# Attention and expert kernel: start-up transfers, an integer block count, a re-ordered last batch and a last block in halves

## The reference

```python
x = layernorm(x + attention(x))          # x: 8 batches of 512 tokens, 128 wide
x = layernorm(x + experts(x))
# attention, 16 heads of 64: linear, no softmax
q, k, v = split(x @ W_qkv);  q, k = relu(q @ W_f + b_f), relu(k @ W_f + b_f)
out = (q @ (k^T @ v)) / (q . sum(k) + 1e-6);  return out @ W_out + b_out
# experts: 8, two for each token, hidden width 512
p, i = top_2(softmax(x @ gate_w^T))
return sum over the two of  p * (gelu(x @ w1[i] + b1[i]) @ w2[i] + b2[i])
```

## Time and profile before

| | |
|---|---|
| median of 3 runs | 463.35 us (462.35 to 464.86) |
| profiled execution | 462.59 us, span 460.8 us |
| busy share PE, DVE, ACT, POOL | 93%, 71%, 60%, 35% |
| chain that ended last | PE 77%, DVE 11% |

### The profile page before, as it was taken

One profiled execution on the slowest core, in us unless ns is written; L12 is line 12 of the kernel. 1 busy time (PEld: TensorE's weight loads), 2 busy tenths in 40 slices (PEclk: granted clock), 3 DMA queues, 4 the chain that ended last, 5 costly groups with the idle time before them and its releaser, 6 DMA issues.

```text
span 460.8 us, 8851 instructions
## 1 busy us (share of the span) xinstructions
PE 429.2 (93%) x2784; PEld 342.2 (74%) x2784; DVE 325.5 (71%) x946; ACT 274.4 (60%) x538; POOL 162.3 (35%) x164
## 2 busy tenths in 40 slices
PE   6989999999999999999999979889999999999940
PEld 5876776776776776776776647569999999999840
DVE  3574968969968968969968997755874433456786
ACT  2664766756756756756656636339555565555565
POOL 2011101431431431431431402425777655555550
PEclk9899999999999999999999999999999999999985
DMA  8980220210210210210100060499696899499534
GB/s 221 303 213 0 71 68 1 74 43 2 69 43 6 70 41 7 68 43 7 60 29 7 24 230 24 142 310 297 192 245 217 280 359 302 130 355 329 165 125 137
DMA packets 40013, 61.16 MB, mean 133 GB/s; under 512 B 6287, under 2 KB 27284, under 8 KB 39840
## 3 DMA queue, kind: packets, MB, share of 16 engines
q1 hardware_dynamic: 30560, 49.65, 34.4%
q0 software_dynamic: 4544, 8.54, 5.3%
q10 hardware_dynamic: 4864, 2.42, 1.8%
HBM read 44.55 MB, written 17.49 MB: 135 GB/s over the span
## 4 chain that ended last, share of the span: by engine, by line
PE 77%; DVE 11%; issue 3%; DMA 3%; ACT 2%; ACTq 1%; POOL 1%; SPq 1%; POOLq 0%; DVEq 0%
PE psO L575 11%; PE psA L465 9%; PE psA L466 9%; PE psA L467 9%; PE psG L705 7%; PE psA L554 6%; PE psS L705 4%; PE psG L465 3%; PE psA L622 3%; PE psG L566 3%; PE psG L466 3%; PE psG L467 3%; PE psG L597 2%; PE psS L511 1%; DMA rn<-expert_rows 1%
## 5 line engine op out<-in xcount | busy, mean ns | idle before, releaser
L425 POOL DMA_INDIRECT expert_rows<-rows,pos x64 | 62.1, 970 | 95.9 <-PE psA L467 67.0
L450 POOL DMA_INDIRECT expert_results<-q_act,kT x56 | 55.4, 989 | 44.5 <-DVE q_act L1213 33.5
L726 ACT ACTIVATE kT<-psA,bf_col 128x512 f32<-128x512 f32 x64 | 44.0, 688 | 37.9 <-PE psA L467 37.5
L575 PE MATMUL psO<-qn,mixed 128*128 128x512 f32 x128 | 64.0, 593 | 0.0
L726 ACT ACTIVATE q_act<-psA,bf_col 128x512 f32<-128x512 f32 x64 | 44.1, 689 | 25.9 <-PE psA L467 25.3
L893 DVE TENSOR_TENSOR k_lo<-psA,k_hi 128x512 fp32r<-128x512 f32 x64 | 43.9, 686 | 7.0 <-ACT k_hi L726 6.3
L1124 DVE TENSOR_TENSOR qn<-q_act,psG 128x512 f32<-128x512 f32 x64 | 42.9, 680 | 8.2 <-PE psG L566 8.2
L705 PE MATMUL psG<-x_raw,q_act 128*128 x384 | 46.9, 275 | 0.3 <-ACT q_act L867 0.2
L705 PEld LDWEIGHTS psG<-x_raw,q_act 128*128 128x128 f32 x384 | 44.9, 192 | 0.7 <-issue 0.7
L554 PEld LDWEIGHTS psA<-cst,kT 128*128 128x128 f32 x256 | 32.0, 142 | 17.4 <-issue 5.8
L465 PE MATMUL psA<-xT_hi,wk_hi 128*128 128x512 f32 x64 | 41.5, 649 | 2.8 <-POOL xT_lo L416 2.8
(11 more groups left out here) (199 smaller groups left out, 1044.0 us busy)
## 6 DMA issues: line engine op xcount, KB each, us to landing
k_hi<-expert_weights SPq DMA_DIRECT2D x15, 578.0 KB
k_lo<-expert_weights SPq DMA_DIRECT2D x15, 578.0 KB, 5.4
w_more<-expert_weights SPq DMA_DIRECT2D x9, 578.0 KB, 4.7
expert_weights<-w_more SPq DMA_DIRECT2D x8, 512.0 KB, 2.9
kT<-expert_rows SPq DMA_DIRECT2D x28, 132.0 KB, 4.5
w_raw<-w SPq DMA_DIRECT2D x8, 256.0 KB, 3.4
x_raw<-w SPq DMA_DIRECT2D x1, 2048.0 KB, 9.2
x<-expert_results SPq DMA_DIRECT2D x4, 512.0 KB, 6.3
```

The lines of the kernel that those rows point to most:

```text
L425: pool.indirect_dma_start(xs, bass.IndirectOffsetOnAxis(ap=pos_2[o % 2][:, j, k:k + 1], axis=0), rows_2[o % 2][:, j, k, :], None).then_inc ...
L450: pool.indirect_dma_start(ys, bass.IndirectOffsetOnAxis(ap=xrow[r][:, c, D:D + 1].bitcast(I32), axis=0), yrow[u][:, c, :], None, bounds_ch ...
L575: mm(psO[:, :], mixed[:, c, :], qn[:, c % 4, :], start=c == 0, stop=c == CH - 1).then_inc(o_pe, 1)
L726: return act.activation(out_, in_, func, **kw)
```

## The change

- ACT's three last start-up issues (constants, gate weights, output bias) move to SP, behind its third load. The casts of constants on DVE move from the start into chunk 4 of call 0.
- `count` becomes an integer add of 255, a shift by 8 and a cast.
- `early_table(0)` to `(3)` stand in chunks 0, 2, 4 and 6 of call 7, `early_table(4)` behind the chunks.
- In each seam `mark` goes behind L1187, `ranks` behind two of the four token tiles of `gram(1)`, and ACT rounds r_hi and r_rest by halves.
- In call 7 `norms` stands one token tile earlier, and `weigh`, `place` and `mixed_second` go into chunks 3, 5 and 2 of call 8.
- `store` waits for each half alone. The last block's second layer writes its two halves into two banks and signals after each; `last_result(c)` finishes them one at a time. `last_means(5)` and `(6)` stand behind the last result and share one chain with group 4.

```diff
-STAT_AT = {30: 0, 32: 1, 34: 2, 36: 3, 38: 4, 39: 5, 40: 6}
-CHAIN_AT = {37: ((0, 4),), 40: ((4, 6), (6, 7))}
+STAT_AT = {30: (0,), 32: (1,), 34: (2,), 36: (3,), 38: (4,), 40: (5, 6)}
+CHAIN_AT = {37: (0, 4), 40: (4, 7)}
...
             sp.dma_start(wqkvT_sb[:, 0:CH, :], wqkv_v[:, 0:CH, :]).then_inc(in_fold_q, 16)
+            sp.dma_start(cst[:, P:], consts[:, P:_C["spread"][0]]).then_inc(in_c, 16)
+            sp.dma_start(gw[:, :], gwT).then_inc(in_small, 16)
+            sp.dma_start(bout_col[:, :], bout.rearrange("(d a) -> d a", a=1)).then_inc(in_small, 16)
...
-                pool.wait_ge(e_y, n + 1)
                 for c in range(2):
+                    pool.wait_ge((e_y1, e_y)[c], n + 1)
...
-                    gram(0, (0, 1))
+                    ahead = (0, 1) if b < B - 1 else (0,)
+                    gram(0, ahead)
                     norms()
-                    gram(0, (2, 3))
+                    gram(0, range(len(ahead), TILES))
+                    gram(1, (0, 1))
                     if prev:
                         ranks(p)
-                    gram(1, (0, 1, 2, 3))
+                    gram(1, (2, 3))
...
-                        last = mm(psY2[bank_of(n)][:, t, :], hT[v][:, c, t * P:(t + 1) * P], ...)
+                        last = mm(result_at(n, t), hT[v][:, c, t * P:(t + 1) * P], ...)
+                    if n == NBLK - 1 and t == 0:
+                        last.then_inc(e_half, 1)
...
-            act.dma_start(cst[:, P:], consts[:, P:_C["spread"][0]]).then_inc(in_c, 16)
-            act.dma_start(gw[:, :], gwT).then_inc(in_small, 16)
-            act.dma_start(bout_col[:, :], bout.rearrange("(d a) -> d a", a=1)).then_inc(in_small, 16)
...
-                    act.wait_ge(n_step, N_STEPS * (b + 1))
-                    hi(r_hi[:, :], rn[:, 1, :]).then_inc(r_h, 1)
-                    hi(r_rest[:, :], rn[:, 1, :], scale=con("take")[:, 1:2]).then_inc(r_h, 1)
+                    for h in range(2):
+                        half = slice(h * S // 2, (h + 1) * S // 2)
+                        act.wait_ge(n_step, N_STEPS * b + 2 + h)
+                        hi(r_hi[:, half], rn[:, 1, half]).then_inc(r_h, 1)
+                        hi(r_rest[:, half], rn[:, 1, half], scale=con("take")[:, 1:2]).then_inc(r_h, 1)
...
-                tb(dve.tensor_tensor(full[:, 0:n * E, :], ..., ALU.is_gt))
+                tb(dve.tensor_scalar(whole_i[:, rows_, :], hist[:, rows_, :], float(BLK - 1), None, ALU.add))
                 tb.wait()
-                tb(dve.tensor_reduce(upto[:, lo_:lo_ + n, :]..., full[:, 0:n * E, :], AX_X, ALU.add))
+                tb(dve.tensor_scalar(whole_i[:, rows_, :], whole_i[:, rows_, :], 8, None, ALU.logical_shift_right))
+                tb.wait()
+                tb(dve.tensor_copy(upto[:, rows_, :], whole_i[:, rows_, :]))
...
+                    if b == B and c == 2:
+                        mixed_second(B - 1)
+                    if b == B and c == 3:
+                        routers[B - 2].weigh()
+                    if b == B and c == 5:
+                        routers[B - 2].place()
...
-                    if b == B - 1 and 1 <= c <= 5:
-                        early_table(c - 1)
+                    if b == B - 1 and c % 2 == 0:
+                        early_table(c // 2)
...
+            def last_result(c):
+
+                n = NBLK - 1
+                u, r = n % SLOTS, n % ROW_SLOTS
+                dve.wait_ge((e_half, e_down)[c], (1, n + 1)[c])
+                dve.wait_ge(e_out[(n - SLOTS) % ROW_SLOTS], 32 * ((n - SLOTS) // ROW_SLOTS + 1))
+                dve.tensor_tensor(yrow[u][:, c, :], result_at(n, c), b2_bc[n % W_SLOTS][:, c, :], ALU.add).then_inc(e_y0, 1)
+                dve.wait_ge(e_y0, n + 1 + c)
+                dve.scalar_tensor_tensor(yrow[u][:, c, :], yrow[u][:, c, :], xrow[r][:, c, D + 1:D + 2], xrow[r][:, c, 0:D],
+                                         ALU.mult, ALU.add).then_inc((e_y1, e_y)[c], 1)
```

More of the change, by code:

```diff
@@ L188, in program @@
         hist = sb("hist", [1, 5, E])
-        full = sb("full", [1, 3 * E, 16])
+        whole_i = sb("whole_i", [1, 5, E], I32)
         upto = sb("upto", [1, 5, E])
@@ L237, in bank_of, with result_at @@
             return n % 2 if n >= PAIRED else 0
+        def result_at(n, t):
+            return psX2[bank_of(n)][:, 0:D] if n == NBLK - 1 and t else psY2[bank_of(n)][:, t, :]
         def before(n):
@@ L1116, in attention @@
                 p = b - 1
-                router = Router(p)
+                router = routers[p] if cur and prev else None
                 def normalise(c):
@@ L1155, in attention @@
                             lo(w1_split[ex % 2][:, F:], w1_raw[ex % 2], w1_split[ex % 2][:, 0:F]).then_inc(w1_l, 1)
+                    if b == 0 and c == 4:
+                        dve.wait_ge(in_c, 16)
+                        dve.wait_ge(in_ident, 16)
+                        dve.tensor_copy(ones_b[:, :], con("ones")).then_inc(cast, 1)
+                        dve.tensor_copy(tri_b[:, :], con("tri")).then_inc(cast, 1)
+                        dve.tensor_copy(base[:, :], con("first")).then_inc(cast, 1)
                     if b == 0 and c == 6:
@@ L1239, in _ @@
                     dve.scalar_tensor_tensor(xT_lo[:, at], psX2[bank_of(n)], 2.0, xT_hi[:, at].bitcast(F32), ALU.mult, ALU.subtract).then_inc(e_Tl, 1)
-                if n >= 2:
+                if 2 <= n <= NBLK:
                     result(n - 2)
+                if n == NBLK + 1:
+                    for c in range(2):
+                        last_result(c)
                 if n == 1:
@@ L1256, in _ @@
                     late_table(n - 6)
-                if n in STAT_AT:
-                    last_means(STAT_AT[n], range(TILES), f_in[STAT_AT[n]])
+                for g in STAT_AT.get(n, ()):
+                    last_means(g, range(TILES), f_in[g])
                 if n in CHAIN_AT:
-                    for groups in CHAIN_AT[n]:
-                        last_chain(*groups)
+                    last_chain(*CHAIN_AT[n])
             for h in range(2):
@@ L1264, in _ @@
             last_chain(B - 1, B)
[L1265 removed]
+            dve.wait_ge(f_ln, LN_STEPS * 3)
             for t in range(2, TILES):
```

34 lines of the change are left out of this document (16 added, 18 removed).

## The result

The changed kernel takes 456.06 us (455.49 to 456.45, 4 runs) beside 462.85 (461.30 to 464.86, 4 runs) of the kernel before: a ratio of 0.987 (0.984 to 0.990). Its profiled execution has a span of 453.7 us in place of 460.8. I predicted 455.5, in a range of 453.4 to 458.6.

What follows compares the result with a forecast made beforehand. PE's own work bounds the regular calls, so gains lie where PE waits. Terms -3.5 - 2.8 - 0.6 + 0.3 - 0.25 - 0.55 = -7.4 us took 462.59 to 455.2; forecast 455.5, range 453.4 to 458.6.

Steps and rivals of the forecast that it cites:

- Start: Start-up: earlier table load brings first key product 2.4 us forward, full clock saves 1.5; 3.5 us taken (2.1 to 3.9).
- Call 7: Chunks of call 7: shorter count 0.5, last table part moved 1.34, new stand of parts 1.0; 2.8 us less (1.8 to 3.9).
- the new stand of the parts: Call 7: PE can do all but the last product while DVE is at the 0.9 us part; 1.0 us less.
- Regular seams: Seams between calls: L1066 moved behind L1187 saves 0.3 us in each of two calls; 0.6 us less (0 to 0.8).
- Last seam: Last seam: rounding by halves starts no earlier and adds two instructions; 0.3 us lost (0 to 0.4).
- Moved work in call 8: Call 8: moved weigh, place and copy fit DVE's free time; later scatters leave POOL 2.7 us idle; 0 us.
- Blocks: Expert blocks: the first half's own wait starts POOL's gapless run earlier, shortening PE's wait for rows; 0.25 us less (0 to 0.49).
- Tail: After the last block: group 5's statistics leave the last result's path, last store issued 0.84 us earlier; 0.55 less (0.4 to 0.84).
- Rival 2: Call 7: DVE stays the bound and only the removed work counts, 1.8 us, total 456.5; chance 0.1.
- Rival 1: Start: only the shift, 2.1 instead of 3.5 us, as clock falls or a load holds; 456.9; chance 0.15.
- Rivals 3 and 4: Late scatters push POOL, 456.5 at 1 us too late, chance 0.05; first x rows land late, slower, chance 0.02.

Runs made afterwards that it cites:

- e12: Changed kernel, table parts 1 and 2 at chunks 1 and 2 of call 7, third behind ksd, fourth and fifth behind last seam's reciprocals: 455.03 us, 0.984.
- e11: Kernel before, 11 matmuls of zeros put on PE behind the fold products, in its idle time ahead of the first key product: 488.42 us, 1.001.
- e5: Changed kernel run again unaltered, beside later runs: 456.20 us, 0.987.
- e10: Kernel before, only the table's last part moved, from chunk 5 of call 7 to behind ksd: 486.19 us, 0.997.
- e6: Changed kernel, table's first part in chunk 1 of call 7 instead of chunk 0: 455.53 us, 0.986.
- e2: Changed kernel, r_hi and r_rest rounded whole again instead of by halves: 481.06 us, 0.995.
- e7: Changed kernel, table's five parts back at chunks 1 to 5 of call 7, new short count kept: 458.82 us, 0.993.
- e8: Changed kernel, last block and last statistics as before, store's first half still waiting for itself alone: 457.00 us, 0.988.
- e3: Changed kernel, the three start-up issues back on ACT's queue, moved casts kept: 483.01 us, 1.000.
- e4: Kernel before, 20 matmuls of zeros put on PE behind the fold products, ahead of the first key product: 484.78 us, 1.003.

## Why the prediction was right, term by term

The terms miss by +0.3 us in all: call 7 by +0.9, the tail and the last seam by +0.5, and against them the blocks by -0.7, the start and the regular seams by -0.4. That the sum of 7.4 came so near to 7.10 is in good part luck. So is the forecast of 455.5: -7.4 from the median of 463.35 is 455.95, and I added only 0.3 of the 0.76 between that median and the profiled execution.

- **Start, -3.5: measured -3.73.** The shift was 2.56 for my 2.4, in this execution; in others with the same start it was less, down to 0.7 (e12). The clock fell for the reason named, the pause, and not in its absence (e11). Its price was mis-sized: 0.8 us where I had 1.5, because PE, freed of it, runs into the wait for k_lo. That wait, 0.4 us behind casts on DVE, I had priced at nothing, and that the change moves the casts as well was luck: both together give 1.44 (31.52 to e5's 30.08). The identity's load, for which I took 0.4 off, held PE for 0.44 us in the changed kernel and not in e5; the front took 30.35 and 30.08.
- **Call 7, -2.8: measured -1.91. This is the step that failed**, although the total came out. The last part's 1.34 was right (1.33 in e10), `count`'s 0.5 nearly (0.24 to 0.4). Of the 1.0 for the new stand of the parts 0.2 to 0.3 was left. I had looked at what stands between which DVE steps, but not at what POOL does at that moment: part 0 in chunk 0 meets x_lo, and 0.56 us are lost (e6). Without that loss the stand would have brought 0.7 to 0.9, near my 1.0.
- **Regular seams, -0.6: measured -0.75.** Right, by the port that I didn't name.
- **Last seam, +0.3: measured +0.47.** The two instructions cost 0.28 (e2; 0.35 forecast). The Trainium skill, "VectorE: DVE Perf Modes", "The TRN2 errata", has a fixed cost that makes 0.37 of them, an estimate, and the trace is below it. 0.19 more is lost ahead of `mix`, where `norms` now stands one token tile earlier: PE has 0.15 us of idle time ahead of it there, and none in the kernel before. No run tested that.
- **Moved work in call 8, 0: measured -0.01.** The late scatters ended at 303.26 and POOL's first store had 2.96 us of idle time before it (2.7 forecast).
- **Blocks, -0.25: measured -0.96.** Block 18 was turned 4.10 us behind block 17 before and 3.44 now, so about 0.7 us of waiting for its rows vanished; in e5 a wait of 0.7 stands at block 20, in e7 and e8 0.5 and 0.9 at block 18, in e12 none. It is the landing of rows, a matter of the execution, and my 0.25 can't be told from it. The other 0.3 are elsewhere: PE waited 0.32 us for xT_lo at 426.71 in the kernel before, and no longer does. No run tested why.
- **Tail, -0.55: measured -0.21, and 0.03 of it from the last block and the statistics (e8).** Mis-sized: I took POOL's issues for constant at 1.28 us apart. The first of the last four came 0.29 us earlier, counted from the turn of block 37, as I had it; but the third follows the second by 1.63 us, and the last is only 0.46 earlier instead of 0.84. The remaining 0.18 of ACT's last step, the store's own wait or chance, wasn't told apart.

Rival 2 (1.8 in call 7) was nearer than my 2.8 there, and in part for its reason: PE still waited 0.83 us for DVE's k_lo ahead of the last transposes. Rival 1 (start only 2.1) did not come in the trace of the changed kernel. Rivals 3 and 4 did not come: the late scatters had ended, and x_hi waited for nothing.

## What to carry to other kernels

Ask of a VectorE instruction that takes several times as long as its neighbours what GpSimd does at the same time; moving it by one chunk, 2.5 us, was worth 0.56 us here, more than a shorter `count`. Work on a bound engine belongs behind the last reader that PE waits for, and next to a wait of that engine. And a PE wait of 2 us can cost more than its length, because it may take the clock down with it: 1.67 us more in call 7 here.

## What the runs showed of the hardware

- DVE steps of 0.17 to 0.19 us took 1.05 to 1.19 us beside a POOL subtraction of 128x512, and ended 0.02 to 0.05 us behind it.
- PE's clock after a pause: low after 2.81 (before) and 2.72 us (e3), after 2.15 to 2.16 us in three executions of four (e4, e7, e11, not in the kernel before), full after 2.01 us (e10).
- The same program takes 20 us more on some chips, in the expert blocks. In e2, on such a chip, PE, DVE and ACT stood for stretches of 1.1 to 6.6 us between 299.7 and 306.3, and SP's issues came 2.8 and 2.9 us apart where they are 1.1 to 1.3 apart in the changed kernel, while transfers and POOL's issues went on:

```profile
...
306.29 0.89 DVE L1106 BATCH_NORM_STATS2 stats<-psO 128x6 f32<-128x128 f32 x4 [6.56 <-remote]
306.33 0.38 ACT L738 ACTIVATE xT_hi<-psG 128x256 fp32r<-128x256 f32 x1 [2.16 <-remote]
...
```

The same DVE step begins at 300.24 in the changed kernel, 1.9 us after the one before it. What holds the engines there stays open.
